# An attention and expert block on one core: GpSimd's roots and residual additions, the scaling of z, the last pair's order and the first pair's banks are moved

## The reference

```python
x = x + attention(layernorm(x))        # 4 batches, 1024 tokens, width 128, 16 heads of 64
x = x + experts(layernorm(x))          # 8 experts, each takes at most 512 tokens

def attention(x):
    q, k, v = x @ w_q, x @ w_k, x @ w_v          # per head
    z = softmax(q @ k.T / 8) @ v
    return x + concat(z) @ w_o                   # the layernormed x is added again here

def experts(x):
    probs = softmax(x @ Wr); e = argmax(probs); p = probs[e]
    rank = number of earlier tokens with the same e; keep = rank < 512
    return scatter(keep * p * (relu(x @ W1[e]) @ W2[e]))
```

## Time and profile before

| | |
|---|---|
| runs | 1545.63, 1541.67, 1545.32 us, median 1545.32 |
| the profiled execution | 1542.72 us, of which 1541.0 us are the span |
| mean granted TensorE clock | 0.985 of full speed |
| PE / PEld busy | 1492.5 / 868.5 us |
| DVE / ACT / POOL busy | 1012.7 / 800.0 / 1202.7 us |
| DMA | 144.14 MB, mean 94 GB/s |
| chain that ended last | PE 87%, POOL 5%, DVE 4%, issue 2% |

### The profile page before, as it was taken

One profiled execution on the slowest core, in us unless ns is written; L12 is line 12 of the kernel. 1 busy time (PEld: TensorE's weight loads), 2 busy tenths in 40 slices (PEclk: granted clock), 3 DMA queues, 4 the chain that ended last, 5 costly groups with the idle time before them and its releaser, 6 DMA issues.

```text
span 1541.0 us, 22167 instructions
## 1 busy us (share of the span) xinstructions
PE 1492.5 (97%) x7538; PEld 868.5 (56%) x7538; DVE 1012.7 (66%) x1228; ACT 800.0 (52%) x1573; POOL 1202.7 (78%) x667
## 2 busy tenths in 40 slices
PE   7999999999999999999999999999999999999796
PEld 4455555555555555655555555555555556554576
DVE  6566666766677666766667666767667667676632
ACT  3556555555555555555555454555565646454321
POOL 3689887888777777888777777888877989979425
PEclk8999999999999999999999999999999999999899
DMA  5334344433443434333444433323343533330430
GB/s 145 79 76 96 100 104 123 103 98 85 99 100 91 105 84 100 83 72 80 96 100 95 103 89 94 92 71 78 91 100 88 137 83 94 80 88 24 145 128 38
DMA packets 126031, 144.14 MB, mean 94 GB/s; under 512 B 44330, under 2 KB 69423, under 8 KB 125920
## 3 DMA queue, kind: packets, MB, share of 16 engines
q1 hardware_dynamic: 119008, 132.36, 35.4%
q0 software_dynamic: 2560, 6.14, 1.1%
q10 hardware_dynamic: 4352, 4.23, 0.9%
HBM read 18.91 MB, written 12.65 MB: 20 GB/s over the span
## 4 chain that ended last, share of the span: by engine, by line
PE 87%; POOL 5%; DVE 4%; issue 2%; DMA 1%; ACT 1%; SPq 1%; POOLq 0%; DVEq 0%; ACTq 0%
PE ps_w L1295 27%; PE ps_w L1281 16%; PE ps_w L1282 14%; PE ps_m L1239 10%; POOL acc L575 3%; PE ps_m L1221 3%; PE ps_m L1328 3%; PE ps_w L1313 2%; PE ps_m L1212 2%; PE ps_m L1213 2%; PE ps_m L1214 2%; DVE mxw L979 1%; PE ps_w L1567 1%; PE ps_m L1567 1%; PE ps_w L1587 1%
## 5 line engine op out<-in xcount | busy, mean ns | idle before, releaser
L575 POOL TENSOR_TENSOR acc<-acc,ring 128x1024 f32<-128x1024 f32 x382 | 919.3, 2407 | 50.9 <-ACT ring L744 3.3
L979 DVE TENSOR_REDUCE mxw<-ps_m 128x1 f32<-128x1024 f32 x508 | 598.1, 1219 | 384.3 <-PE ps_m L1239 383.1
L744 ACT ACTIVATE ring<-ps_w 128x512 f32<-128x512 f32 x1024 | 545.0, 597 | 241.8 <-PE ps_w L1282 238.0
L1295 PE MATMUL ps_w<-ring,V 128*64 128x512 f32 x2048 | 470.4, 601 | 0.0
L1281 PE MATMUL ps_w<-queriesA,keysA 128*128 128x512 f32 x1024 | 432.4, 422 | 1.1 <-DMA queriesB<-mxt 0.7
L1282 PE MATMUL ps_w<-queriesB,keysB 65*128 65x512 f32 x1024 | 407.0, 397 | 0.0
L575 POOL TENSOR_TENSOR acc<-ring 128x1024 f32<-128x1024 f32 x64 | 151.8, 2373 | 183.5 <-PE ps_w L1313 171.5
L1295 PEld LDWEIGHTS ps_w<-ring,V 128*64 128x64 f32 x2048 | 136.3, 137 | 267.8 <-issue 227.1
L1281 PEld LDWEIGHTS ps_w<-queriesA,keysA 128*128 128x128 f32 x1024 | 194.5, 190 | 89.4 <-issue 46.7
L1282 PEld LDWEIGHTS ps_w<-queriesB,keysB 65*128 65x128 f32 x1024 | 194.9, 190 | 34.3 <-issue 0.7
L1239 PE MATMUL ps_m<-keysA,queriesA 64*128 64x512 f32 x1016 | 188.7, 449 | 8.8 <-DVE x L999 3.0
(11 more groups left out here) (167 smaller groups left out, 938.5 us busy)
## 6 DMA issues: line engine op xcount, KB each, us to landing
queriesA<-qk_high SPq DMA_DIRECT2D x248, 128.0 KB, 2.4
keysB<-qk_high SPq DMA_DIRECT2D x124, 128.0 KB, 2.4
keysA<-qk_rest SPq DMA_DIRECT2D x124, 128.0 KB, 2.4
queriesB<-qk_rest SPq DMA_DIRECT2D x124, 128.0 KB, 2.3
by_sums<-sums SPq DMA_DIRECT2D x240, 64.0 KB, 2.0
keysA<-qk_high SPq DMA_DIRECT2D x93, 128.0 KB, 2.4
tokens_by_slot<-blank ACTq DMA_DIRECT2D x16, 258.0 KB, 3.6
ring<-tokens_by_slot SPq DMA_DIRECT2D x8, 516.0 KB, 7.4
```

What stands on the lines that cost most here:

```text
L575: pool.tensor_tensor(acc[h][:, :], before, P_both(kt), ALU.add).then_inc(summed, 1)
L744: act.activation(P_tile(kt, p), ps_s[k % 3][:, :], ACT.Exp, scale=SCALE).then_inc(exp_done, 1)
L979: dve.tensor_reduce(mxw[h][:, p * HT + qt:p * HT + qt + 1], ps_v[banks][p], AX_X, ALU.max).then_inc(maxed, 1)
L1295: mm = pe.matmul(ps_z[p * DK:(p + 1) * DK, :], V[par][:, kt * P + p * DK:kt * P + (p + 1) * DK], P_tile(kt, p), start=(kt == 0), stop=(kt ...
```

## The change

Five things move; the arithmetic stays. Line numbers below the first part are two lower on VectorE, and up to two lower on TensorE, in the changed kernel.

1. **GpSimd**: `inverse_root` of a batch moves from half 1 of the pair ahead to before the first addition of the batch-numbered pair, `residual` from half 0 of that pair to before the first addition of the pair after it; the router's `inverse_root` likewise. ScalarE's `first_norm` and `copy_hT`, and TensorE's turns, follow one oct or so later.
2. **VectorE**: `scale_z` stands behind the second reductions of its oct rather than between the first ones and the rest.
3. **First pair**: the second half of the first queries goes to `ps_z`, `turn_max` and V's second half to `ps_s[0]`; `low_first(6, ...)` moves from before pair 0 into its oct 0; TensorE waits for `first_low` 4 only at `values`.
4. **Last pair**: `values` ahead of `end_turn`; the sums over the last two key tiles are split around the logits.
5. **Spins**: 12 new ones before the last turns; 64, a wait for the last scatter and 20 more in place of 40.

```diff
-        first_q = [ps_m[1][:, 0:HALF], ps_s[0]]
+        first_q = [ps_m[1][:, 0:HALF], ps_z]
@@ gpsimd, pair
-                        if early(j, 1) is not None and (h, kt) == (1, 1):
-                            inverse_root(early(j, 1))
-                        if early(j, 0) is not None and (h, kt) == (0, 5):
-                            residual(early(j, 0))
-                        if routed(j, "a") is not None and (h, kt) == (1, 5):
-                            inverse_root(B + routed(j, "a"))
+                        if early(j, 0) is not None and (h, kt) == (0, 1):
+                            inverse_root(early(j, 0))
+                        if early(j, -1) is not None and (h, kt) == (0, 1):
+                            residual(early(j, -1))
+                        if routed(j, "b") is not None and (h, kt) == (0, 1):
+                            inverse_root(B + routed(j, "b"))
@@ scalar, pair
-                    if early(j, 0) is not None and oct in (1, 2):
-                        copy_hT(early(j, 0), oct - 1)
+                    if early(j, 0) is not None and oct >= 2:
+                        copy_hT(early(j, 0), oct - 2)
-                    if early(j, 1) is not None and oct == 3:
-                        first_norm(early(j, 1), 0)
-                    if early(j, 0) is not None and oct == 0:
-                        first_norm(early(j, 0), 1)
+                    if early(j, 0) is not None and oct < 2:
+                        first_norm(early(j, 0), oct)
@@ vector, pair
-                    if oct == 0 and j >= 2:
-                        scale_z(j - 2, 1)
-                    if oct == (0 if last else 3) and not first:
-                        scale_z(j - 1, 0)
...
+                        low_first(6, first_q[1], queriesA, [queriesB[0][0], first_rest_q], slice(HALF, S))
...
                         reduce_max(v, h, qt, 1)
                         reduce_max(v, h, qt, 0)
+                    if oct == 0 and j >= 2:
+                        scale_z(j - 2, 1)
+                    if oct == (0 if last else 3) and not first:
+                        scale_z(j - 1, 0)
@@ vector, start
-            low_first(6, first_q[1], queriesA, [queriesB[0][0], first_rest_q], second_half)
-            low_qk(1, 0)
             for p in (1, 0):
                 reduce_max(4, 1, 0, p)
+            low_qk(1, 0)
@@ tensor
-                    pe.wait_ge(first_low, 4)
+                    pe.wait_ge(first_low, 2)
...
+                if oct == 0 and j == 0:
+                    pe.wait_ge(first_low, 4)
...
+                    values(j, par, oct)
                     if last and oct == 3:
                         end_turn(0, 0)
                         end_turn(0, 1)
-                    values(j, par, oct)
@@ tensor, start
-            turn_max(0, 0, lent_max)
+            project_v(0, 0, 0, 0, ps_s[2])
+            turn_max(0, 0, ps_s[0])
+            pe.wait_ge(first_cast, 8)
+            max_scores(4, 0, 1, 0)
             project_qk(1, 1, 0, 0)
-            pe.wait_ge(first_cast, 8)
             pe.wait_ge(c_copied, 1)
-            max_scores(4, 0, 1, 0)
-            project_v(0, 0, 0, 0, ps_s[2])
-            project_v(0, 0, 1, 0, ps_z)
+            project_v(0, 0, 1, 0, ps_s[0])
             max_scores(5, 0, 1, 1)
@@ tensor, end
+            sums_by_pe(LAST, 1, range(KT - LAST_BY_PE, KT - 1))
             make_logits(B - 1, lent_out, range(HT))
-            sums_by_pe(LAST, 1, LAST_BY_PE)
+            sums_by_pe(LAST, 1, range(KT - 1, KT))
...
+            spin(12, ps_s[2])
             for k in range(2):
                 end_turn(1, k)
...
-            spin(40)
+            spin(64)
+            pe.wait_ge(scattered[B - 1], 16 * QT)
+            spin(20)
```

More of the change, by code:

```diff
@@ L1189, in _, with spin @@
             pe.wait_ge(dve_consts, 4)
-            def spin(times):
+            def spin(times, bank=ps_z):
                 for _ in range(times):
-                    pe.matmul(ps_z[:, 0:P], ident[:, :], ident[:, :], start=True, stop=True)
+                    pe.matmul(bank[:, 0:P], ident[:, :], ident[:, :], start=True, stop=True)
             def turn_h(b, g):
@@ L1298, in values, with sums_by_pe @@
                 mm.then_inc(pv_done, 1)
-            def sums_by_pe(j, h, by_pe):
-                for kt in range(KT - by_pe, KT):
+            def sums_by_pe(j, h, tiles):
+                for kt in tiles:
                     for p in range(2):
                         pe.matmul(sums_bank(j, h)[p * DK:(p + 1) * DK, :], ones[:, :], P_tile(kt, p),
-                                  start=(kt == KT - by_pe), stop=False)
+                                  start=(kt == KT - LAST_BY_PE), stop=False)
             def softmax_sums(j, h, by_pe=0):
@@ L1405, in pair @@
                     all_out = 16 * j + 12 + 4 * oct
-                    turn = (early(j, 0), oct - 1) if early(j, 0) is not None and oct in (1, 2) else None
+                    turn = (early(j, 0), oct - 2) if early(j, 0) is not None and oct >= 2 else None
                     c = routed(j, "c")
```

7 lines of the change are left out of this document (3 added, 4 removed).

## The result

The changed kernel took 1541.7 us in the median of 12 runs (1538.3 to 1544.3) and the kernel before, on the same chip, 1544.7 us (12 runs): a ratio of 0.998, 95% interval 0.9971 to 0.999, so about 3 us faster. In two later sets of runs it came to 0.9985 (0.9974 to 0.9996) and 0.9971 (0.9959 to 0.9983). The forecast was 1536 us: a sum of -7.6 us, and 9 us under the median of the three runs shown before. The time lies in the range; the gain is less than half of the one forecast, and inside the 0.3% that the prediction counts as no change.

What follows compares the result with a forecast made beforehand. TensorE, busy for 97% of the span, was taken as the bound, so only its waits and slow stretches could give time. Terms 9.4 - 10.2 - 4.0 - 2.8 = -7.6 us took 1542.72 to 1535.1, forecast as 1536 us, range 1526 to 1546.

Steps and rivals of the forecast that it cites:

- The first pair, +9.4: First pair: SyncE's queue 8.3 us late delays TensorE's visit 7.9 us, plus 1.5 us of slow clock; bounds +7 to +12.
- Pairs 0 to 2, -10.2: Pairs 0 to 2: softmax sums' 7.2 us of waits for GpSimd go, with slow stretches behind them; -8 to -11 us.
- The cover: GpSimd's waits for the softmax sums, 6.1 us each, under which the moved root and residual addition, 6.7 us, would fall.
- Mid-run, -4.0: Mid-run, oct 3: TensorE's visit comes 0.32 us behind the scores, not 0.50, in some 22 pairs; bounds 0 and -5 us.
- the scaling ends a microsecond early: Mid-run on VectorE: the moved scaling ends at 949.4, a microsecond before the next reductions start at 950.36.
- Pairs 30 and 31, -1.6: Pairs 30 and 31: the 2.25 us stop goes, but TensorE meets GpSimd at pair 31's half 0 sums; 1.6 us gained.
- the first rival: VectorE's scaling is caught behind a GpSimd addition, TensorE loses 1.4 us in some 27 pairs: 1573 us; chance 0.08.
- The end, -1.2 of the -2.8: After the last scores: 4.8 us gained, 84 spins of 18.8 us as the bound, expert phase at full clock worth -1.5 us.
- The harmless queue: Rival, first pair: SyncE's late queue does no harm, so the +9.4 us cost does not come: 1525.7 us; chance 0.10.
- the missing early gain: Rival, pairs 0 to 2: the root holds ScalarE's first_norm or GpSimd is late again, no -10.2 us: 1545.3 us; chance 0.12.
- The slow end: Rival, end and pair 0: spins at the slow clock first, and a longer slow stretch in pair 0: 1539 us; chance 0.15.
- The caught scaling: Rival, mid-run: the scaling waits behind a GpSimd addition and delays the next reductions 1.6 us: 1573 us; chance 0.08.

Runs made afterwards that it cites:

- e1: Changed kernel with the two subtractions of low_first(6, ...) back ahead of reduce_max(4, ...), all else as changed: 0.9934 of the kernel before.
- e5: Kernel before with only the roots and residual additions moved, and the ScalarE and TensorE places that follow them: 0.9935 of the kernel before.
- e13: Kernel before with only the new end (values' order, split sums, 12 spins, then 64, wait, 20): 1.0002 of the kernel before.
- e6: Kernel before with only the scaling's new place on VectorE: 0.9968 of the kernel before.
- a_third: Changed kernel repeated unedited, in the fourth set of runs: 0.9971 of the kernel before.
- a_again: Changed kernel repeated unedited, in the second set of runs: 0.9985 of the kernel before.
- e9: Changed kernel with pair 29's first scaling one oct sooner and GpSimd's four last scatters in half 1 of pair 31: 0.9979 of the kernel before.
- e8: Changed kernel with 40 spins at the end and no wait or spins behind them: 0.9947 of the kernel before.
- e2: Changed kernel with 40 spins, the wait, then 12 at the end, in place of 64, wait, 20: 0.9931 of the kernel before.

## Why the prediction was right and wrong

- **The first pair, +9.4: right, with some luck in the number.** +9.0, +9.6 and +10.3 in three executions, by the mechanism named: SyncE's DMA at 36.92, the cast's wait of 8.04 us, the slow visit. e1 gives 7 us back by moving two instructions. But of the two terms the delay of the visit was 6.8 us in the first execution (7.1 and 7.9 in the others) for the 7.9 forecast, and the slow clock cost 2.2 to 2.6 us for the 1.5 forecast. The other moves ahead of pair 0, which the prediction took for hidden, are hidden only behind this stop: e1 shows 1.5 us of them.
- **Pairs 0 to 2, -10.2: right.** The offset moves by -9.8 to pair 3 and e5 alone measures -10.0 (-7.4 to -12.5). The waits are gone, 7.2 us. The 3.0 us of slow clock in the forecast are what this one execution of the kernel before lost; e13 lost nothing at the same waits, e6 3.4 at the second. The cover that the prediction named, GpSimd's waits before the first sums, holds.
- **Mid-run, -4.0: right.** e6 is 4.2 us early at pair 27, the changed kernel's step is 3.5 in the mean. The visit comes at 0.32 us, and the scaling takes 0.87 us for the 0.9 forecast. But the part "the scaling ends a microsecond early" was too sure for the late pairs: from pair 27 to 30 the changed kernel gives back 1.3 us (e6 0.6), where GpSimd scatters tokens and stands differently to VectorE. One scaling there, and TensorE behind it:

```profile
1252.22 2.84 DVE L991 TENSOR_TENSOR z<-by_sums,z 128x512 f32<-128x512 f32 x1
...
1256.25 0.50 PE L1210 MATMUL ps_m<-h_high,w_low 128*128 128x512 f32 x1 [0.54 <-DVE mxw L977]
```

- **Pairs 30 and 31, -1.6: wrong, about 0.** The wait for GpSimd came where the text put it, at the sums of pair 31's half 0, and at 2.6 us it was longer than the "one to two". What I left out was its price: I had put 1.4 to 1.5 us of slow clock on the stops of the first pairs, and none on the stop that I predicted myself. It costs 1.7 to 3.4 us by the windows, and undoes the 1.6 (e6: 3.6 early at pair 30, 3.5 at the last copy). In one execution of three the first rival's mechanism took this wait's place, a scaling of 3.65 us and a stop of 3.05 with some 5 us of slow clock behind it. The prediction did not see that the same scaling had already been held in the kernel before, for 3.60 us.
- **The end, -1.2 of the -2.8: wrong, about 0.** e13 measures +0.3 (-1.9 to +2.3). What the new order gives up to the ranks was right: 4.8 forecast, 4.7 measured (5.2 less the 0.5 by which the scores ended sooner). The failed term is 84 spins at 0.224 us, 18.8 us: they took 21.0, 21.1 (a_third) and 20.6 us (e13) by their rows. The price of a spin at full clock was right; the clock was not full. It was at 0.50 for the first 4.2 us of the spins in the first execution, which costs 2.1 us, and for 3.4 us of them in e13 and a_again, in spite of the 12 spins meant to keep it. The price of a spin at a slow start stood in the earlier trace rows, 0.29 for the 40 of before; I used it for a bound only.
- **The rivals.** The harmless queue and the missing early gain are refuted by e1 and e5. The slow end is nearest to what happened. The caught scaling did not come in mid-run, but its mechanism is real. A scaling that is caught lasts until 0.55 to 0.6 us behind the end of GpSimd's addition: 0.87 us where the addition is nearly over, 2.6 to 3.65 where it has just begun, and 0.68 alone; the four rows of e9 show it. The Trainium skill (GPSIMD Engine Reference, section 2, Architecture) states one physical read port to SBUF that both engines share; the traces agree, and show beside it a scaling of 0.68 us during a scatter by GpSimd (a_again).

By the single parts the sum is -10.0 (e5), -5 (e6), +0.3 (e13) and the first pair's +9.6 (from the offsets): -5.1 us, against -3.3 for the mean of the whole kernel's three ratios. The 1.8 us between them is inside the intervals of these runs, and what of it is the parts' effect on each other stays open, as does e8's distance to e2.

## What to carry to other kernels

When a wait is removed and the next one is named, price that next one in full: its length and the slow clock behind it. Before an instruction is moved past a queue, look at who waits for that queue with an engine's wait already showing on it; here two subtractions of 0.69 us cost 7 us. Before a gain is read off one profile, look at whether its slow stretches come back in a second one. Work that keeps an engine awake has to be shorter than what it covers, counted at the clock it will start with.

## What the runs showed of the hardware

- The same scaling of 128x512 takes 0.68 us alone or beside a scatter by GpSimd (a_again). Behind an addition of 128x1024 it lasts until 0.55 to 0.6 us after that addition's end: 0.87 us in mid-run, 2.68 and 2.85 in e9, 3.65 in the changed kernel. At one place it was caught with 0.02 us in hand (the changed kernel) and let through with 0.03 (e5), so that one kernel shows two different stops in pair 31 from one execution to the next.
- A stop of 2.6 us for TensorE at a granted clock of 1.00 was followed by ten microseconds at 0.66 in e2 and 0.83 in a_again: the same stop has prices that differ by 1.7 us. Behind the stop of 3.05 us TensorE was busy without a break for 9.2 us at a granted clock of 0.50 (1393.8 to 1403.0).
- The wait for GpSimd at the second softmax sums stands in a window, 130 to 140, whose granted clock was 0.83 in the kernel before, 1.00 in e13 and 0.75 in e6, three kernels whose programs are the same up to there but for a scaling's place. With the first sums (0.91 and 0.92 over 80 to 100, 1.00 in e13) the clock cost the kernel before 3.4 us more than e13, which is 2.3 us ahead of it at pair 3.
- The tail from the tokens' turns on took 76 to 77.5 us in one set of runs and 71 to 73 in the others, for code that is the same there but for its spins: a last phase like this is to be compared within one set only.
